# Graph convolutions: 126 of every 128 edge rows gathered by GpSimd, the last two fetched by SyncE

## The chip, the cores and the metric

The kernel runs on one core of a Trainium2 chip. The metric is the device time of one execution in microseconds (us). Engines are named as in the profile: PE is TensorE, DVE is VectorE, ACT is ScalarE, POOL is GpSimd and SP is SyncE; a "q" behind a name (SPq, POOLq) is the sequencer of that engine, which issues transfers, loads registers and waits.

## The reference

There are N = 6250 nodes with D = 512 features and E = 100000 edges, sorted by destination. First comes a graph attention layer, then two graph convolution layers, each of this form (W is 512x512):

```python
h = x @ W
deg = segment_sum(ones, dst) + 2.0
dinv = rsqrt(deg)
msgs = h[src] * (dinv[src] * dinv[dst])[:, None]
agg = segment_sum(msgs, dst) + h * (2.0 * dinv * dinv)[:, None]
x = relu(agg + b)
```

So each of the two convolutions has to read one row of 512 floats (2 KB) for each of the 100000 edges, by the edge's source, and to add it to the row of the edge's destination.

## The kernel before

The nodes are 49 tiles of 128 rows. The edges are J = 782 chunks of P = 128 edges; two chunks are a unit, and there are UNITS = 391 units. A convolution is two stages. A dense stage (`dense_layer`, L1561) makes x @ W tile by tile, already scaled, and SP writes it to a table in HBM (`h2_tab` for the first convolution, `h3_tab` for the second; the profile calls both h_tab), L1164. Then comes the aggregation stage, in which this change lies:

- **POOL** (`gather`, L1286 to L1303) issues one indirect transfer per chunk. It brings 128 rows of the table, named by a column of `src_group`, into one slot of `gcn_ring`, one row for each of the 128 partitions. The ring holds RING[1] = 12 units, which is 24 slots or six pairs of units. From the seventh pair on POOL waits, before each pair, until PE has used the pair six earlier (`step_sum`). The step numbers to wait for come from `ends_row`, 16 of them in one register load (L1293). The profile puts the gathers down to L1301.
- **SP** (`count_rows`, L1113 to L1118) waits for each pair's transfers (`rows_in`, one semaphore for each of the six places of the ring) and adds two to `rows_ready`.
- **ACT** (`make_group_onehots`) makes one-hot matrices of the destinations, for groups of four steps.
- **PE** (`aggregate`, L1713 to L1731) works through 440 steps (a constant that the code, too, calls SP); a step is one unit against one tile of destinations, so there are 49 more steps than units. Before each group of four steps it waits for `rows_ready` (that all units of the group have landed) and for the one-hots. Each step is a matmul of 128x128 by 128x512 in fp32 for each of its two chunks, which the profile shows as four records.
- **DVE** (L909) adds the finished steps to the accumulators in SBUF. In the second aggregation it also finishes tiles, and ACT writes them out and loads rows of `x1_tab` (L1530, L1536).

Before the first aggregation SP issues the loads of two biases and of the second weight matrix (L1179 to L1183); before the second it issues twelve loads of 256 KB each from `x1_tab` (L1196). During the two aggregations it has nothing to do but `count_rows`. The attention stage has a gather of the same kind (from v_tab), and that call isn't touched.

Of the kernel before, what the change touches and what calls it, by code (L numbers as in the profile page):

```python
# [8 lines left out]
I32 = mybir.dt.int32  # L9
# [3 lines left out]
ds = bass.ds  # L13

P = 128
# [3 lines left out]
TILES = -(-N // P)  # L19
NP = TILES * P  # L20
LAST = N - (TILES - 1) * P
J = -(-E // P)
# [24 lines left out]
UNITS = J // 2  # L47
# [5 lines left out]
SP = CUT.steps  # L53
# [4 lines left out]
ENDS = 16  # L58
LAG = 2
OFFS = 8  # L60
WORD = 1023
# [32 lines left out]
W_EXTRA = 2 * GE * H  # L94
XR = 4
SHORT = 3
SETTLED = UNITS
BIG = 1e38
EPS = 1e-5
# [30 lines left out]
def build(nc, x, src, dst, W_src, b_src, W_dst, b_dst, W_val, b_val, attn_l, attn_r, W1, b1, W2, b2, out):  # L130
    ctx = ExitStack()
    with ctx:
        def sb(name, shape, dt=F32):
            return ctx.enter_context(nc.sbuf_tensor(name, shape, dt))
# [4 lines left out]
        def sem(name):  # L139
            return ctx.enter_context(nc.semaphore(name))  # L140

        def dram(name, shape, dt=F32):
            return nc.dram_tensor(name, shape, dt, kind="Internal").ap()


        src_rows = dram("src_rows", [GROUPS, GE], I32)
# [13 lines left out]
        h2_tab = dram("h2_tab", [NP, D])  # L160
        h3_tab = dram("h3_tab", [NP, D])
# [31 lines left out]
        eler_hots = sb("eler_hots", [P, TILES * 2 * H])  # L193
# [3 lines left out]
        ends_row = sb("ends_row", [1, UNITS + 1], I32)  # L197

        src_group = sb("src_group", [P, J], I32)
# [24 lines left out]
        gcn_ring = edge[:, 0:2 * RING[1] * D].rearrange("p (s n) -> p s n", n=D)  # L224
# [3 lines left out]
        onehot = hots[:, :].rearrange("p (b c n) -> p b c n", b=HOTS, c=2)  # L228
        group_hots = hots[:, :].rearrange("p (g e n) -> p g e n", g=HOTS // GROUP, n=P)
        dist = eler_hots[:, 0:4 * P].rearrange("p (b c n) -> p b c n", b=2, c=2)  # L230
        stat = big[:, TILES * D:TILES * (D + 6)].rearrange("p (t s) -> p t s", s=6)
        ln = small[:, 0:4, :]
        iota_i = small[:, 4:7, :].rearrange("p s t -> p (s t)")[:, 0:P].bitcast(I32)
        W_src_sb = wmat[:, :, 0:D]
        rows = rows_w[:, :, 0:D]
# [96 lines left out]
        def first(t):  # L332
# [15 lines left out]
        ends_kept, tabs_kept, tabs_in, chunks_in = map(sem, ("ends_kept", "tabs_kept", "tabs_in", "chunks_in"))  # L348
        pad_set, const_set, ident_set, edges_kept, fold_in, edges_in, dst_in = map(sem, (
            "pad_set", "const_set", "ident_set", "edges_kept", "fold_in", "edges_in", "dst_in"))  # L350
# [12 lines left out]
        v_kept = [sem(f"v_kept{n}") for n in range(4)]  # L363
        el_in = [sem("el_in0"), sem("el_in1")]
        stepdst_in = sem("stepdst_in")
        er_in, w_kept = map(sem, ("er_in", "w_kept"))
# [3 lines left out]
        lasts_in, counted, elerT_set, eler_turned = map(sem, ("lasts_in", "counted", "elerT_set", "eler_turned"))  # L370
# [5 lines left out]
        ht_kept, low_before = low_in, [16 * len(range(n, KEPT, HT)) for n in range(HT)]  # L376
        gcn_rows_in = [sem(f"gcn_rows_in{u}") for u in range(RING[1] // 2)]
        gat_rows_in = [sem(f"gat_rows_in{u}") for u in range(RING[0])]
        agg = []
        for n, (name, c) in enumerate((("gat", 0), ("gcn1", 1), ("gcn2", 1))):  # L380
            units = RING[c]
            agg.append(dict(
                units=units, told=1 + c,
                rows_in=(gat_rows_in, gcn_rows_in)[c],
                rows_before=[32 * (n == 2) * sum(1 for g in range(UNITS) if g % units // 2 == u) for u in range(units // 2)]
                if c else [0] * units,
                rows_ready=sem(f"{name}_rows_ready"),
                dist_set=sem(f"{name}_dist_set"), onehot_set=sem(f"{name}_onehot_set"),
                step_sum=sem(f"{name}_step_sum"), acc_added=sem(f"{name}_acc_added")))
# [7 lines left out]
        mids = []  # L397
# [21 lines left out]
        def all_kept(eng, pair, per=16):  # L419
            eng.wait_ge(pair[0], per * ((TILES + 1) // 2))  # L420
            eng.wait_ge(pair[1], per * (TILES // 2))
# [3 lines left out]
            eng.wait_ge(w_placed_odd, 2 * CUT.blocks)  # L425

        waits_passed = {eng: sem(f"waits_passed_{eng}") for eng in ("pool", "dve")}

        def wait_alone(name, eng, which, value):

            eng.wait_ge(which, value)
            eng.sem_inc(waits_passed[name], 1)
# [11 lines left out]
        def _(dve):  # L444
# [513 lines left out]
            def residual(s):  # L958
                first_tiles = not s.inner and s.k < SHORT + 3
                if s.live():  # L960
                    begin_tile(s)
                if s.live(1):
                    tile_moments(s.k - 1, (s.j - 1) % 2)
                if first_tiles and 1 <= s.k <= SHORT:
                    tile_scale(s.k - 1, (s.k - 1) % 2, s.k >= 3)
                if s.live(2) and not (first_tiles and s.k - 2 < SHORT):
                    tile_scale(s.k - 2, s.j % 2, s.past(2, 2))
                if first_tiles and 2 <= s.k < SHORT + 2:
                    bank_out(mids[0], s, 2)
                if not (first_tiles and s.k - 3 < SHORT):  # L970
                    bank_out(mids[0], s, 3)
# [37 lines left out]
            def settled(k):  # L1009

                t = k - LAG - SETTLED
                if 0 <= t - 1 < TILES:
# [4 lines left out]
            dve.wait_ge(agg[2]["acc_added"], SP)  # L1017
            for k in range(SP + LAG - 1, SETTLED + LAG + TILES + 1):
                settled(k)
# [8 lines left out]
        def _(sp):  # L1028
# [32 lines left out]
            for t in range(TILES):  # L1061
                sp.wait_ge(hT_set, t + 1)
                if STAY_LO <= t < STAY_HI:
                    n = t - STAY_LO
# [48 lines left out]
            def count_rows(a):  # L1113

                for g in range(0, UNITS, a["told"]):
                    u, told = g % a["units"] // a["told"], min(a["told"], UNITS - g)
                    sp.wait_ge(a["rows_in"][u], a["rows_before"][u] + 32 * (g // a["units"] * a["told"] + told))
                    sp.sem_inc(a["rows_ready"], told)  # L1118

            def load_low(s):  # L1120
                if s.past(4):
                    sp.wait_ge(src_hot_set, (s.k - 3) * (KT - 1))
                    sp.wait_ge(far_dist, s.k - 3)
                if not s.inner and s.k in ER_LOAD:
                    n = ER_LOAD.index(s.k)
                    at = slice(n * J * H // 4, (n + 1) * J * H // 4)
                    if n == 0:
                        all_landed(sp, er_scattered, TILES)
                    sp.wait_ge(v_sum, STAY_LO)
                    sp.dma_start(er.rearrange("p j h -> p (j h)")[:, at],  # L1130
                                 er_tab[0:EP, :].rearrange("(p j) h -> p (j h)", j=J)[:, at]).then_inc(er_in, 16)
                sp.dma_start(low_all[:, s.j, :], low_tab[ds(s.k * Q, Q), :].rearrange("q n -> (q n)").rearrange(
                    "(a n) -> a n", a=1).broadcast_to([P, Q * P])).then_inc(low_in[s.j], 16)
# [4 lines left out]
            for half, at in enumerate(halves):  # L1138
                at = slice(at.start * H, at.stop * H)
# [45 lines left out]

            all_kept(sp, x1_kept)

            count_rows(agg[1])

            def between(s):  # L1190
                keep_table(mids[1], h3_tab, s, 0)
# [2 lines left out]
            sp.wait_ge(b_added, TILES)  # L1194
            for t in range(EARLY_X1):
                sp.dma_start(x1_buffer(t), x1_tab[t * P:(t + 1) * P, :]).then_inc(x1_early_in, 16)  # L1196
            count_rows(agg[2])
            sp.wait_ge(out_kept, 16 * TILES)


# [1 line left out]
        def _(pool):  # L1202
# [29 lines left out]
            for g in range(TILES // SEEK):  # L1232
# [3 lines left out]
                for t in range(g * SEEK, (g + 1) * SEEK):  # L1236
                    pool.indirect_dma_start(seek_ring[:, t % (2 * SEEK), :], None, by_row, bass.IndirectOffsetOnAxis(
                        ap=er_idx[:, t:t + 1], axis=0)).then_inc(seek_in[g % 2], 16)
# [27 lines left out]
            for t in range(TILES):  # L1266
# [8 lines left out]
                ap=dst_i[:, 0:1], axis=0)).then_inc(er_first_in, 16)  # L1275
# [7 lines left out]
                pool.indirect_dma_start(w_row_of[b], None, w_tab,  # L1283
                                        bass.IndirectOffsetOnAxis(ap=gidx[:, b:b + 1], axis=0)).then_inc(w_in[b], 16)

            def gather(tab, a, ring, done):  # L1286

                units, ends = a["units"], None
                for g in range(UNITS):
                    u, past = g % units, g - units  # L1290
                    if past >= 0:
                        if past % ENDS == 0:
                            _, ends = nc.values_load_multi_w_load_instructions(  # L1293
                                ends_row[:, past:min(past + ENDS, UNITS - units)], engines=(mybir.EngineType.Pool,),
                                min_val=1, max_val=SP, skip_runtime_bounds_check_because="clamped when the table is made")
                        if past % a["told"] == 0:
                            freed = min(past % ENDS + a["told"], len(ends)) - 1
                            wait_alone("pool", pool, done, ends[freed] & WORD)
                    for c in range(2):
                        n = 2 * g + c  # L1300
                        pool.indirect_dma_start(  # L1301
                            ring[:, 2 * u + c, :], None, tab,
                            bass.IndirectOffsetOnAxis(ap=src_group[:, n:n + 1], axis=0)).then_inc(a["rows_in"][u // a["told"]], 16)  # L1303

            pool.wait_ge(tabs_in, 64)
            pool.wait_ge(dve_prep, marks["tables"])
# [16 lines left out]
                    collect_den(t + XR)  # L1323
            pool.wait_ge(x1_set, TILES)
            all_kept(pool, mids[0]["kept"])
            gather(h2_tab, agg[1], gcn_ring, agg[1]["step_sum"])
            all_kept(pool, mids[1]["kept"])
            gather(h3_tab, agg[2], gcn_ring, agg[2]["step_sum"])


        @block.scalar
        def _(act):
# [166 lines left out]
            def residual(s):  # L1499
                first_tiles = not s.inner and s.k < SHORT + 2  # L1500
                if s.live(1):
# [36 lines left out]
            def settled(q):  # L1538
                for t in range((q - 4) * GROUP - SETTLED, (q - 3) * GROUP - SETTLED):
                    if 0 <= t < TILES:  # L1540
                        out_and_x1(t)
            make_group_onehots(agg[2], settled)
            for t in range((SP // GROUP - 4) * GROUP - SETTLED, TILES):
                out_and_x1(t)
# [233 lines left out]
```

## Time and profile before

| what | value |
|---|---|
| device time, three runs | 4063.41, 4064.51 and 4065.05 us, median 4064.51 us |
| profiled execution | 4065.91 us, of which 4064.1 us are its span (first to last instruction) |
| busy shares of the span | PE 85%, POOL 66%, DVE 55%, ACT 44% |
| gathers of the two convolutions (L1301, h_tab) | 1564 of them, 1482.5 us busy, 948 ns each |
| first aggregation, its gathers | from 1856.69 us on, 782 of them |
| second aggregation, its gathers | from 3046.16 us on, the last one issued at 4026.08 us |
| all DMA | 789.67 MB, mean 194 GB/s |

The page shows the span in 40 slices of about 102 us. Slices 19 to 28 are the first aggregation, slices 31 to 40 the second. In them POOL's digit is 7, PE's is 8, and DMA moves 210 GB/s. A busy share isn't yet a bound: for each stage one has to ask who waits for whom, and at what interval the instructions of the slowest engine start. Times of one instruction are in ns.

### The profile page before, as it was taken

The numbers are of one execution on the slowest core, as the hardware profiler recorded it, in microseconds if no ns is written. First come the engines' busy times: TensorE is split into PE (matmuls) and PEld (weight loads), VectorE is DVE, ScalarE is ACT, GpSimd is POOL, SyncE is SP. The second block draws the span as 40 slices with busy tenths as digits, with TensorE's granted clock in tenths as the row PEclk, the third lists the DMA queues.
The fourth block names the chain that finished last, engine by engine and source line by source line (L and its number), as shares of the span: only waits on it lengthen the run. The fifth ranks groups of instructions, "written<-read, shape, count | busy, mean of one in ns | idle before, by whom it ended". The sixth has DMA issues, their size and how long they took to land.

```text
span 4064.1 us, 53477 instructions
## 1 busy us (share of the span) xinstructions
PE 3446.4 (85%) x14344; PEld 1653.5 (41%) x14344; DVE 2246.1 (55%) x3787; ACT 1789.0 (44%) x4164; POOL 2666.3 (66%) x2801
## 2 busy tenths in 40 slices
PE   6899998777888888897788888889996788888887
PEld 4499943222233333443333333333442333333333
DVE  7489997777778888882223323333542222223336
ACT  4356615454455555453334434444443333334442
POOL 3676604777777777555777777776007777777774
PEclk9999999999999999998999999999998999999998
DMA  7633437777777777566777777776117777777779
GB/s 278 165 65 62 94 109 244 210 211 211 210 210 210 211 210 210 186 204 194 210 210 210 211 210 210 210 211 192 60 70 238 211 210 210 210 210 210 210 210 352
DMA packets 311566, 789.67 MB, mean 194 GB/s; under 512 B 74033, under 2 KB 97091, under 8 KB 310449
## 3 DMA queue, kind: packets, MB, share of 16 engines
q0 software_dynamic: 201856, 631.01, 54.3%
q1 hardware_dynamic: 81813, 108.37, 8.4%
q10 hardware_dynamic: 27708, 48.21, 3.4%
q8 instruction: 66, 1.08, 0.1%
q14 instruction: 123, 1.01, 0.1%
HBM read 706.27 MB, written 81.90 MB: 194 GB/s over the span
## 4 chain that ended last, share of the span: by engine, by line
PE 34%; POOL 24%; issue 21%; DMA 12%; DVE 6%; POOLq 1%; DVEq 1%; ACT 1%; ACTq 0%; SPq 0%
POOL edge L1301 18%; PE mm L1561 8%; POOL rows_wmat L1301 6%; DMA edge<-h_tab,src_group 5%; DMA rows_wmat<-v_tab,src_group 5%; PE mm L1729 4%; PE mm L1657 4%; PE tr L1657 4%; PE sm L1729 4%; PE tr L1729 3%; PE sm L1602 2%; DVE edge L882 2%; PE tr L1556 1%; PE hist_ps L1729 1%; DVE big L894 1%
## 5 line engine op out<-in xcount | busy, mean ns | idle before, releaser
L1301 POOL DMA_INDIRECT edge<-h_tab,src_group x1564 | 1482.5, 948 | 708.8 <-issue 447.2
L1468 ACT ACTIVATE hots<-iota,drel 128x128 f32<-128x128 f32 x1760 | 538.0, 388 | 1174.8 <-PE tr L1729 578.2
L1301 POOL DMA_INDIRECT rows_wmat<-v_tab,src_group x782 | 739.3, 945 | 258.8 <-issue 219.3
L1729 PE MATMUL mm<-edge,hots 128*128 x880 | 448.7, 658 | 185.7 <-SPq L1118 177.1
L1729 PE MATMUL sm<-edge,hots 128*128 x880 | 460.8, 673 | 158.3 <-SPq L1118 158.3
L909 DVE TENSOR_TENSOR big<-big,mm 128x512 f32 x220 | 151.2, 687 | 658.9 <-PE tr L1729 639.9
L909 DVE TENSOR_TENSOR big<-big,sm 128x512 f32 x220 | 151.2, 687 | 630.9 <-PE misc L1729 616.9
L1729 PE MATMUL tr<-edge,hots 128*128 x880 | 395.6, 592 | 0.0
L1729 PEld LDWEIGHTS mm<-edge,hots 128*128 128x128 f32 x880 | 177.1, 209 | 450.1 <-issue 450.1
L1729 PEld LDWEIGHTS sm<-edge,hots 128*128 128x128 f32 x880 | 182.7, 215 | 428.3 <-issue 428.2
L1561 PE MATMUL mm<-rows_wmat 128*128 128x512 f32 x784 | 356.6, 599 | 0.0
L1709 PE MATMUL mm<-edge,hots 128*128 128x512 f32 x592 | 277.3, 608 | 59.0 <-ACT hots L1450 39.3
L1709 PE MATMUL sm<-edge,hots 128*128 128x512 f32 x584 | 275.9, 602 | 54.9 <-issue 28.3
L882 DVE TENSOR_TENSOR edge<-rows_wmat,tr 128x1024 f32<-128x1024 f32 x224 | 272.0, 1215 | 81.9 <-SPq L1118 80.2
L882 DVE TENSOR_TENSOR edge<-rows_wmat,misc 128x1024 f32<-128x1024 f32 x216 | 262.6, 1216 | 80.7 <-SPq L1118 80.6
L1450 ACT ACTIVATE hots<-eler_hots,ones 128x256 f32<-128x256 f32 x440 | 223.6, 508 | 186.7 <-PE sm L1709 68.1
L1445 ACT ACTIVATE eler_hots<-iota,drel 128x128 f32<-128x128 f32 x880 | 298.2, 386 | 0.0
L1260 POOL DMA_INDIRECT edge<-el_tab,src_flat x222 | 212.6, 958 | 99.7 <-issue 56.1
L1471 ACT ACTIVATE hots<-hots,ones 128x1024 f32<-128x1024 f32 x220 | 252.6, 1148 | 7.1
L1729 PEld LDWEIGHTS tr<-edge,hots 128*128 128x128 f32 x880 | 167.6, 190 | 212.3 <-issue 212.3
L1729 PE MATMUL hist_ps<-edge,hots 128*128 x440 | 206.8, 592 | 0.0
L1729 PE MATMUL misc<-edge,hots 128*128 x440 | 206.8, 592 | 0.0
(262 smaller groups left out, 4424.8 us busy)
## 6 DMA issues: line engine op xcount, KB each, us to landing
h_tab<-rows_wmat SPq DMA_DIRECT2D x98, 256.0 KB, 2.0
edge<-h_tab,src_group POOLq DMA_INDIRECT x1564, 3.7
rows_wmat<-low_tab SPq DMA_DIRECT2D x140, 128.0 KB
v_tab<-rows_wmat ACTq DMA_DIRECT2D x49, 256.0 KB, 2.9
x_tab<-big SPq DMA_DIRECT2D x49, 256.0 KB, 2.1
rows_wmat<-v_tab,src_group POOLq DMA_INDIRECT x782, 3.7
edge<-x SPq DMA_DIRECT2D x48, 256.0 KB
out<-big ACTq DMA_DIRECT2D x48, 256.0 KB
```

The source lines that it names most:

```text
L882: dve.tensor_tensor(msgs[:, k % MSGS, :, :].rearrange("p c (h f) -> p c h f", f=F), got, weights.unsqueeze(3).to_broadcast([P, 2, H, F]), ...
L909: dve.tensor_tensor(big[:, ds(o, D)], big[:, ds(o, D)], agg_ps[bank][:, :], ALU.add).then_inc(a["acc_added"], 1)
L1260: pool.indirect_dma_start(el[:, at, :], None, el_tab, bass.IndirectOffsetOnAxis(ap=src_flat[:, at:at + 1], axis=0)).then_inc(el_in[n // AH ...
L1301: pool.indirect_dma_start(ring[:, 2 * u + c, :], None, tab, bass.IndirectOffsetOnAxis(ap=src_group[:, n:n + 1], axis=0)).then_inc(a["rows_ ...
L1445: act.activation(dist[:, n % 2, c, :], iota[:, :], ACT.Abs, bias=drel[:, n * 2 + c:n * 2 + c + 1], scale=-1.0).then_inc(a["dist_set"], 1)
L1450: act.activation(onehot[:, n % HOTS, :, :], dist[:, n % 2, :, :], ACT.Relu, bias=ones[:, 0:1], scale=-1.0).then_inc(a["onehot_set"], 1)
L1468: act.activation(group_hots[:, q % 2, e, :], iota[:, :], ACT.Abs, bias=drel[:, col:col + 1], scale=-1.0).then_inc(a["dist_set"], 1)
L1471: act.activation(group_hots[:, q % 2, :, :], group_hots[:, q % 2, :, :], ACT.Relu, bias=ones[:, 0:1], scale=-1.0).then_inc(a["onehot_set"], 1)
L1561: last = nc.tensor.matmul(bank, rows[:, slot, k * P:(k + 1) * P], rhs(k), start=(k == 0), stop=(k == KC - 1))
L1657: last = pe.matmul(sum_ps[bank][:, q * NA * H:(q + 1) * NA * H], src_hot[:, par, kt, q * P:(q + 1) * P], el_parts[:, part, kt, :, :], star ...
L1709: last = pe.matmul(gat_ps[w % GAT_SUMS][:, :], onehot[:, w % HOTS, n, :], msgs[:, w % MSGS, n, :], start=(n == 0), stop=(n == 1))
L1729: last = pe.matmul(agg_ps[bank][:, :], group_hots[:, q % 2, w % GROUP * 2 + n, :], edge[:, ds(slot[w % OFFS] + n * D, D)], start=(n == 0), ...
```

## The change

In both convolutions POOL's indirect transfer brings only the first 126 rows of a chunk (partitions 0 to 125). SP fetches the rows of partitions 126 and 127 with one plain transfer each, whose source row is a register. For this SP loads the sources of the last two edges of every chunk from HBM into one partition (`own_ids`, in two halves of 392 and 390 chunks, the second in the middle of a stage), and from there loads them into registers, eight for a pair of units. `fetch(k)` issues the eight transfers of pair k; from the seventh pair on it first waits, as POOL does, until PE has used the pair six earlier. `relay(k)` takes the place of `count_rows`: it waits for POOL's transfers and for SP's own, and then adds to `rows_ready`. SP does four fetches ahead, and then relay(k) and fetch(k + 4) in turn. The semaphores of its own transfers are ones that earlier stages had used.

```diff
+BY_SYNC = 2
+BY_POOL = P - BY_SYNC
+PAIRS_AHEAD = 4
+UNIT_PAIRS = -(-UNITS // 2)
+IDS_HALF = J // 2 + 1
...
+        own_ids = eler_hots[0:1, 0:IDS_HALF * BY_SYNC].bitcast(I32)
...
+            def fetch_and_count_rows(a, tab, again):
+
+                pairs = a["units"] // 2
+                chunk_src = src_rows.rearrange("g (c e) -> (g c) e", e=P)
+                halves_in, ends_held, ends = [2 * again], [-1], [None]
+
+                def load_ids(half):
+                    lo = half * IDS_HALF
+                    n = min(IDS_HALF, J - lo)
...
+                        sp.dma_start(own_ids[:, 0:n * BY_SYNC].rearrange("a (c e) -> a c e", e=BY_SYNC),
+                                     chunk_src[lo:lo + n, BY_POOL:P].rearrange("(a c) e -> a c e", a=1)).then_inc(ids_in, 16)
+                    halves_in[0] += 1
+                    sp.wait_ge(ids_in, ids_before + 16 * halves_in[0])
+
+                def fetch(k):
+                    first_chunk, chunks = 4 * k, min(4, J - 4 * k)
+                    if first_chunk % IDS_HALF == 0:
+                        load_ids(first_chunk // IDS_HALF)
+                    if k >= pairs:
+                        past = 2 * (k - pairs) + 1
+                        if past // ENDS != ends_held[0]:
+                            ends_held[0] = past // ENDS
+                            _, ends[0] = nc.values_load_multi_w_load_instructions(
+                                ends_row[:, past // ENDS * ENDS:min((past // ENDS + 1) * ENDS, UNITS)],
...
+                        sp.wait_ge(a["step_sum"], ends[0][past % ENDS] & WORD)
+                        sp.sem_inc(waits_passed["sp"], 1)
+                    at = first_chunk % IDS_HALF * BY_SYNC
+                    _, ids = nc.values_load_multi_w_load_instructions(
+                        own_ids[:, at:at + chunks * BY_SYNC], engines=(mybir.EngineType.SP,), min_val=0, max_val=NP - 1,
...
+                    for c in range(chunks):
+                        for e in range(BY_SYNC):
+                            sp.dma_start(gcn_ring[BY_POOL + e:BY_POOL + e + 1, 4 * (k % pairs) + c, :],
+                                         tab[ds(ids[c * BY_SYNC + e], 1), :]).then_inc(own_in[k % pairs], 16)
+
+                def relay(k):
+                    u, turn, told = k % pairs, k // pairs, min(2, UNITS - 2 * k)
+                    sp.wait_ge(a["rows_in"][u], a["rows_before"][u] + 32 * (2 * turn + told))
...
+                    sp.wait_ge(own_in[u], own_before[u] + 16 * BY_SYNC * (before + 4 * turn + 2 * told))
+                    sp.sem_inc(a["rows_ready"], told)
+                for k in range(PAIRS_AHEAD):
+                    fetch(k)
+                for k in range(UNIT_PAIRS):
+                    relay(k)
+                    if k + PAIRS_AHEAD < UNIT_PAIRS:
+                        fetch(k + PAIRS_AHEAD)
...
-            count_rows(agg[1])
+            all_kept(sp, mids[0]["kept"])
+            fetch_and_count_rows(agg[1], h2_tab, 0)
...
-            count_rows(agg[2])
+            fetch_and_count_rows(agg[2], h3_tab, 1)
...
-            def gather(tab, a, ring, done):
+            def gather(tab, a, ring, done, n_rows=P):
...
-                            ring[:, 2 * u + c, :], None, tab,
-                            bass.IndirectOffsetOnAxis(ap=src_group[:, n:n + 1], axis=0)).then_inc(a["rows_in"][u // a["told"]], 16)
+                            ring[0:n_rows, 2 * u + c, :], None, tab,
+                            bass.IndirectOffsetOnAxis(ap=src_group[0:n_rows, n:n + 1], axis=0)).then_inc(a["rows_in"][u // a["told"]], 16)
...
-            gather(h2_tab, agg[1], gcn_ring, agg[1]["step_sum"])
+            gather(h2_tab, agg[1], gcn_ring, agg[1]["step_sum"], BY_POOL)
...
-            gather(h3_tab, agg[2], gcn_ring, agg[2]["step_sum"])
+            gather(h3_tab, agg[2], gcn_ring, agg[2]["step_sum"], BY_POOL)
```

## Rows read from the trace of the kernel before

**Rows 1.** The page: chain that ended last, by engine; gathers' median us to landing.

```profile
PE 34%; POOL 24%; issue 21%; DMA 12%; DVE 6%; POOLq 1%; DVEq 1%; ACT 1%; ACTq 0%; SPq 0%
...
edge<-h_tab,src_group POOLq DMA_INDIRECT x1564, 3.7
```

**Rows 2.** Windows: inside each aggregation, and the second one's last part.

```profile
core 0: us, PE busy (x) PEld busy (x) DVE busy (x) ACT busy (x) POOL busy (x), PEclk, DMA share, GB/s
2000.00:2800.00 800.00, 679.36 (x1458) 285.70 (x1457) 248.47 (x362) 324.85 (x815) 605.04 (x641) 0.95 0.74 210
...
3960.00:4020.00 60.00, 50.69 (x104) 21.07 (x103) 38.86 (x70) 21.60 (x55) 45.97 (x47) 0.90 0.97 360
```

**Rows 3.** POOL's indirect transfers by line, whole span: busy us, mean ns.

```profile
L1301 POOL DMA_INDIRECT edge<-h_tab,src_group x1564 | 1482.5, 948 | 708.8 <-issue 447.2 <-DMA h_tab<-rows_wmat 233.0 <-PE tr L1729 10.4
...
L1260 POOL DMA_INDIRECT edge<-el_tab,src_flat x222 | 212.6, 958 | 99.7 <-issue 56.1 <-DVE rows_wmat L705 30.5 <-DMA el_tab<-eler_hots 13.2
```

**Rows 4.** Timeline of POOL in the second aggregation: start, us.

```profile
3238.70 0.95 POOL L1301 DMA_INDIRECT edge<-h_tab,src_group  x1 [0.30 <-issue]
3239.95 0.94 POOL L1301 DMA_INDIRECT edge<-h_tab,src_group  x1 [0.30 <-issue]
```

**Rows 5.** Line L1283, gathers of 128 rows of 8 KB: ns min/median/max.

```profile
L1283 POOL DMA_INDIRECT big<-w_tab,gidx x2: 1429/1432/1434, 635.4 to 637.1; - x2
```

**Rows 6.** Timeline of PE in the second aggregation, two groups of steps.

```profile
3273.76 3.70 PE L1729 MATMUL mm<-edge,hots 128*128 x8 [2.52 <-SPq L1118]
3277.30 3.60 PE L1729 MATMUL tr<-edge,hots 128*128 x8
3283.75 3.69 PE L1729 MATMUL sm<-edge,hots 128*128 x8 [2.85 <-SPq L1118]
```

**Rows 7.** Waits of SP's sequencer: total us, times, longest.

```profile
SPq L1118 <- DMA edge<-h_tab,src_group: 1937.1, 391, 8.2
```

**Rows 8.** Timeline of SP: transfers into one partition.

```profile
518.91 0.24 SPq L1105 DMA_DIRECT2D ends_row<-ends_tab  x1
519.21 0.25 SPq L1107 DMA_DIRECT2D src_flat<-slot_tab_gat  x1
519.50 0.25 SPq L1107 DMA_DIRECT2D src_flat<-slot_tab_gcn  x1
```

**Rows 9.** Timeline of SP: transfers whose address is a register.

```profile
1696.29 0.35 SPq L1170 DMA_DIRECT2D x_tab<-big  x1
1696.84 0.35 SPq L1153 DMA_DIRECT2D edge<-x  x1
```

**Rows 10.** By line, ns min/median/max: loads of 8 and 16 registers, SP's semaphore instructions.

```profile
L1720 PEldq TENSOR_LOAD <-src_flat x110: 586/589/856, 1848.0 to 4025.9; - x110
L1293 POOLq TENSOR_LOAD <-ends_row x73: 303/1055/1622, 664.3 to 3983.5; - x73
...
L1118 SPq EVENT_SEMAPHORE  x783: 17/17/19203, 645.2 to 4032.2; - x196
```

**Rows 11.** SP before the second aggregation: issues (timeline), time to landing (line).

```profile
3045.92 6.83 SPq L1196 DMA_DIRECT2D rows_wmat<-x_tab  x12
...
DMA to landing us min/median/max: 2.7/7.8/12.7
```

**Rows 12.** Line L1110: issue of a load of 220 single words.

```profile
L1110 SPq DMA_DIRECT2D src_flat<-need_tab x1: 867/867/867, 519.8 to 519.8; - x1
```

**Rows 13.** Timelines: first gather and first matmuls of each aggregation.

```profile
1856.69 0.96 POOL L1301 DMA_INDIRECT edge<-h_tab,src_group  x1 [20.80 <-DMA h_tab<-rows_wmat]
...
1869.31 5.54 PE L1729 MATMUL mm<-edge,hots 128*128 x8 [16.14 <-SPq L1118]
...
3046.16 0.94 POOL L1301 DMA_INDIRECT edge<-h_tab,src_group  x1 [212.17 <-DMA h_tab<-rows_wmat]
...
3061.43 5.11 PE L1729 MATMUL mm<-edge,hots 128*128 x8 [18.20 <-SPq L1118]
```

**Rows 14.** Timelines of the second aggregation's last part: POOL, ACT's sequencer.

```profile
3953.70 1.23 POOL L1301 DMA_INDIRECT edge<-h_tab,src_group  x1 [0.30 <-issue]
3955.24 1.29 POOL L1301 DMA_INDIRECT edge<-h_tab,src_group  x1 [0.30 <-issue]
...
4000.51 2.81 ACTq L1536 DMA_DIRECT2D rows_wmat<-x_tab  x1
```

More of the change, by code:

```diff
@@ L378, in build @@
         gat_rows_in = [sem(f"gat_rows_in{u}") for u in range(RING[0])]
+        own_in, ids_in = v_kept + [w_kept, edges_kept], chunks_in
+        own_before, ids_before = [16 * len(range(n, TILES, 4)) for n in range(4)] + [32, 64], 32
         agg = []
@@ L427, in build @@
         waits_passed = {eng: sem(f"waits_passed_{eng}") for eng in ("pool", "dve")}
+        waits_passed["sp"] = lasts_in
         def wait_alone(name, eng, which, value):
@@ L1118, in count_rows @@
                     sp.sem_inc(a["rows_ready"], told)
+            def fetch_and_count_rows(a, tab, again):
[5 more added lines that the diff above has]
+                    n = min(IDS_HALF, J - lo)
+                    with nc.allow_non_contiguous_dma(reason="sources of the last edges of every chunk"):
+                        sp.dma_start(own_ids[:, 0:n * BY_SYNC].rearrange("a (c e) -> a c e", e=BY_SYNC),
[12 more added lines that the diff above has]
+                                ends_row[:, past // ENDS * ENDS:min((past // ENDS + 1) * ENDS, UNITS)],
+                                engines=(mybir.EngineType.SP,), min_val=1, max_val=SP,
+                                skip_runtime_bounds_check_because="clamped when the table is made")
+                        sp.wait_ge(a["step_sum"], ends[0][past % ENDS] & WORD)
[3 more added lines that the diff above has]
+                        own_ids[:, at:at + chunks * BY_SYNC], engines=(mybir.EngineType.SP,), min_val=0, max_val=NP - 1,
+                        skip_runtime_bounds_check_because="rows of the edges' sources")
+                    for c in range(chunks):
[5 more added lines that the diff above has]
+                    sp.wait_ge(a["rows_in"][u], a["rows_before"][u] + 32 * (2 * turn + told))
+                    before = again * len(range(u, UNIT_PAIRS, pairs)) * 4 - again * 2 * (u == (UNIT_PAIRS - 1) % pairs)
+                    sp.wait_ge(own_in[u], own_before[u] + 16 * BY_SYNC * (before + 4 * turn + 2 * told))
[6 more added lines that the diff above has]
+                        fetch(k + PAIRS_AHEAD)
```

## The prediction

> **What bounds the kernel now.** I read the page's chain first. PE leads it, but POOL and "issue" together have more, 45% [rows 1], so PE's busy share says little by itself. The windows split the aggregation stages from the rest: in 800 us of the first one PE is busy for 679 us and POOL for 605 us, and neither is full [rows 2]. The timeline of POOL settles it: a gather starts every 1.25 us, 0.95 us of work and 0.30 us of "issue", with no wait [rows 4]. Two starts are 1.25 us apart; 782 of them make 977.5 us, which is the length of either aggregation up to its last gather (1564 gathers and their mean: [rows 3]). PE's timeline shows the other side: a group of four steps takes some 7.1 us, and then PE waits 2.5 to 2.9 us for SP's count, with a new group every 10 us [rows 6]. SP in its turn waits for the landing of each pair, 1937 us in all [rows 7]. So the pace is POOL's price for one gather, and a pair of units (four gathers) takes 5.00 us. Is it POOL's own work or the transfer? The gathers from el_tab, in a stage where hardly anything else moves, have the same 0.95 us though their rows are 64 times smaller [rows 3], and the 16 DMA engines are 74% busy beside the gathers [rows 2]. It is POOL's own work.
>
> **What is taken away from POOL.** Two of 128 rows in each of 1564 gathers. No row of the trace shows a gather of fewer than 128 rows, so the saving is bounded. Below: nothing, if the price goes by the instruction. Above: the whole 948 ns go by the row, 2 / 128 of it is 14.8 ns, in all 23 us. Between them lies the nearest price of more work for each row: rows of 8 KB cost 1432 ns [rows 5], 484 ns more than the 948, which is 3.8 ns for each of 128 rows. Two rows fewer at that price save 7.6 ns, times 1564 that is 12 us. I take -12. PE does not cap this: its 7.1 us stand against 10.
>
> **What SP has to do for a pair**, against 5.00 us:
> - A transfer into one partition is issued every 0.29 us [rows 8]. A register as its address adds work: between two such transfers lie 0.55 us from start to start, of which 0.35 us are the first one [rows 9]; 0.05 us of the rest are in the 0.29 already, so 0.15 us come on top. Eight transfers at 0.44 us are 3.52 us.
> - The register load of eight sources: 0.59 us and a gap, 0.64 us; the load of 16 step numbers, 1.06 us, in one pair of eight: 0.14 us [rows 10].
> - Three waits, two semaphore increments and the masking of a step number, at 17 ns each [rows 10] and gaps of about 40 ns: some 0.26 us.
>
> The sum is 4.56 us, so SP keeps up, but with 0.44 us to spare. From both sides: at 0.29 us a transfer (registers free) it is 3.4 us; at the full 0.55 us of the 128-partition form it is 5.4 us. I take 4.56 us, since [rows 8] have the shape, and [rows 9] only the register. What is behind SP: relay(k + 1) stands behind fetch(k + 4), so PE learns of a pair up to 4.6 us late, and PE's steps set the ring free for POOL. In the steady state this is covered: POOL can be 24 gathers (30.0 us) ahead of the pair whose place it wants. A pair is complete 5 us of gathers and 3.7 us of landing [rows 1] after its first gather, may wait 5 us for the rest of its group, and takes up to 7.1 us, 20.8 us together. So SP may be some 9 us behind at no price.
>
> **The start of each aggregation** isn't covered. SP now loads the sources, does four fetches of 4.3 us (without relay), then relay(0), fetch(4) and relay(1), and only then can PE's first group start. Before, it started 12.6 us after the first gather in the first aggregation, 15.3 us in the second [rows 13].
> - First aggregation: the load of 392 pairs of words is issued in about 1.2 us (220 words took 0.87 us [rows 12]) and lands after some 4 us; together 5. Then 17.2 + 4.5 us, and relay(1) is at 26.7 us. PE's first two steps take 5.5 us at its clock after the pause [rows 13]: the first pair's place is free at 32.4 us, and POOL wants it at 30.0 us. Price +2 us, bounds 0 and +7.
> - Second aggregation: the twelve loads of L1196 stand ahead. They are issued at 3052.75 us, 6.6 us after the first gather, and land a median 7.8 us later [rows 11]. The sources land behind them, at about 15.6 us. Then relay(1) is at 37.3 us, and the place is free at 42.5 us. Price +12 us, bounds +8 and +15.
>
> After each of these stalls SP gains 0.44 us on POOL in each pair and has its reserve back after some 20 to 30 pairs. The second half of the sources is loaded in the middle of a stage, some 6 us beside running gathers, inside the 9 us of reserve: +1 for each stage, bounds 0 and +5. In the last 70 us of the second aggregation ACT's stores and loads take the DMA engines to 97% [rows 2], gathers grow to 1.29 us, and an issue on ACT's queue takes up to 2.8 us [rows 14]. SP's 120 small transfers of these pairs go into the same crowd: +3 us, bounds 0 and +10.
>
> **Sum:** -12 + 2 + 12 + 2 + 3 = +7 us on the profiled execution's 4065.9 us, 4072.9 us. The median of the runs lies 1.4 us below that execution, so I predict 4071.5 us. The ends of this case are -23 + 8 = -15 (4049) and 0 + 30, some 4095 us.
>
> **A rule on how the rows are dealt out.** The trace has only 128-row gathers. By the Trainium skill ("DMA: Bandwidth & Descriptors", the section on why a DMA increments its semaphore by 16) a transfer runs on the largest number of engines, up to 16, that divides its slowest dimension. By that rule 128 rows are 8 on each of 16 engines, and 126 rows are 9 on each of 14; and one-partition transfers from SP would all use the lowest-numbered engine. No row here shows either. What each would make of the time is worked out from rows in the second and the fourth rival.
>
> **The rivals.**
> 1. *SP becomes the pace* (slower). It needs 0.495 us a transfer instead of 0.44, since (5.00 - 1.04) / 8 = 0.495; or waits for PE's steps of 0.44 us a pair. At 5.2 us a pair it costs 196 pairs x 2 x 0.2 = 78 us on top of about 17: 4160 us; at the full 0.55 us of [rows 9], 5.4 us, +157 us. For it speak the thin margin, and that fetch(k + 4) needs the steps of pair k - 2, which at times are only the first of the group that relay(k) lets go; against it that [rows 8] show the very shape of transfer. Chance 0.22.
> 2. *A gather of 126 rows costs more than one of 128* (slower). An even deal of 126 rows reaches at most 14 of 16 engines, 9 rows each; if POOL deals evenly and works in waves of one row for each engine, 9 waves take the place of 8. The part that grows with rows is about 484 ns [rows 3, 5]; an eighth of it is 61 ns, x 1564 = +95 us, and with the starts (which then are partly hidden) some 4170 us. For it: 126 isn't a multiple of 16. Against it: nothing in the trace. The rule of the Trainium skill told above gives the same 9 rows, but no time for them. Chance 0.17.
> 3. *A gather gets clearly cheaper* (faster). If the same 484 ns go by the DMA engine served and two of them fall out, the sign is turned: -61 ns, -95 us, and +19 for the rest: 3988 us. SP's 4.56 us a pair would still pass under the 4.76 us that POOL then takes, but barely. It decides from about 17 ns saved in each gather. Chance 0.13.
> 4. *One DMA engine becomes the bound* (slower). The engines are busy for 0.74 of 1.25 us, 0.93 us a gather [rows 2]. If all of SP's rows run on one engine (the rule told above names the lowest-numbered one), it gets two more rows beside its eight: 10 / 8 of 0.93 us is 1.16 us, under 1.25 us, so it shouldn't decide outside the last 70 us. At 1.30 us a gather it would cost 78 us. Chance 0.06.
>
> The forecast's own case, SP keeps up and the gather's price hardly moves, has the remaining 0.42.
>
> **How the numbers follow.** The measurement tells 0.2%, 8.1 us, from no change. The forecast's case (4049 to 4095 us) gives 0.07 to faster, 0.22 to same and 0.13 to slower. With rival 3 faster has 0.20; same has 0.22; with rivals 1, 2 and 4 slower has 0.58. The range leaves out most of rival 3 (0.12) and the far ends of the slow ones (0.08): 4045 to 4180 us.
>
> **What the profile after would show.** The start-to-start time of POOL's gathers in mid-stage: 1.24 us by the forecast; 1.25 or more, or under 1.23, speak for rivals. SP's eight transfers start 0.44 us apart and leave it waiting at the relay for POOL's landing; if it never waits there, and POOL waits for steps throughout, it is rival 1. POOL's seventh pair starts about 2 us late in the first aggregation and 12 us late in the second. The gathers' packets and the busy share of the engines show rivals 2 and 4. I am wrong above all if an issue costs SP over 0.495 us, or if the price of a gather jumps at other than 128 rows in either direction.

## The result, and the profile after

The changed kernel takes 4172.84 us (median of 5 runs, 4168.59 to 4177.62), the kernel before 4064.51 us (5 runs, 4059.89 to 4067.98). The ratio is 1.0266, with an interval of 1.0254 to 1.0278: 108 us slower. The profiled execution has a span of 4171.0 us, 106.9 us more than before.

POOL's rows of the page by line show it at once (busy us and mean ns; compare [rows 3]): the gathers of 126 rows are dearer, not cheaper, while those of 128 rows from v_tab and el_tab cost what they did. There is also idle time before them for which PE is named. The last line is the v_tab row of the kernel before.

```profile
L1362 POOL DMA_INDIRECT edge<-h_tab,src_group x1564 | 1534.8, 981 | 749.9 <-issue 442.2 <-DMA h_tab<-rows_wmat 232.3 <-PE mm L1790 41.9
L1362 POOL DMA_INDIRECT rows_wmat<-v_tab,src_group x782 | 739.4, 946 | 257.9 <-issue 224.5 <-DVE big L864 20.0 <-DVE edge L891 13.4
L1321 POOL DMA_INDIRECT edge<-el_tab,src_flat x222 | 212.7, 958 | 98.8 <-issue 55.8 <-DVE rows_wmat L714 31.1 <-DMA el_tab<-eler_hots 11.8
...
L1301 POOL DMA_INDIRECT rows_wmat<-v_tab,src_group x782 | 739.3, 945 | 258.8 <-issue 219.3 <-DVE big L855 20.9 <-DVE edge L882 18.6
```

POOL's timeline tells where the 107 us are. The rows are, in order: the first gather and the 24th and 25th of the first aggregation, two of its middle, its last; then the first, 24th and 25th of the second, two from its last part, and its last (start us, us; in brackets the idle time before).

```profile
1855.57 1.00 POOL L1362 DMA_INDIRECT edge<-h_tab,src_group  x1 [20.81 <-DMA h_tab<-rows_wmat]
...
1885.15 0.99 POOL L1362 DMA_INDIRECT edge<-h_tab,src_group  x1 [0.30 <-issue]
1893.15 0.97 POOL L1362 DMA_INDIRECT edge<-h_tab,src_group  x1 [7.01 <-PE mm L1790]
...
2301.51 0.97 POOL L1362 DMA_INDIRECT edge<-h_tab,src_group  x1 [0.30 <-issue]
2302.79 0.99 POOL L1362 DMA_INDIRECT edge<-h_tab,src_group  x1 [0.30 <-issue]
...
2865.25 0.99 POOL L1362 DMA_INDIRECT edge<-h_tab,src_group  x1 [0.30 <-issue]
...
3077.69 0.97 POOL L1362 DMA_INDIRECT edge<-h_tab,src_group  x1 [211.45 <-DMA h_tab<-rows_wmat]
...
3107.20 0.99 POOL L1362 DMA_INDIRECT edge<-h_tab,src_group  x1 [0.30 <-issue]
3137.58 0.97 POOL L1362 DMA_INDIRECT edge<-h_tab,src_group  x1 [29.40 <-PE mm L1790]
...
4099.74 0.99 POOL L1362 DMA_INDIRECT edge<-h_tab,src_group  x1 [0.30 <-issue]
4106.53 0.97 POOL L1362 DMA_INDIRECT edge<-h_tab,src_group  x1 [5.80 <-PE sm L1790]
...
4118.44 0.99 POOL L1362 DMA_INDIRECT edge<-h_tab,src_group  x1 [0.30 <-issue]
```

In mid-stage two starts are 1.284 us apart (mean of gathers 300 to 600 of either aggregation) where they were 1.250 us. The 25th gather, the first one that needs a place set free, comes 8.00 us after the 24th in the first aggregation and 30.38 us in the second, which is 6.7 and 29.1 us too late. From the last gather to the end of the span it was 38.0 us, and is 52.6 us. So the 106.9 us divide as follows:

| part | us |
|---|---|
| first aggregation, 781 steps of 34 ns more | +26.6 |
| first aggregation, late 25th gather | +6.7 |
| second aggregation, 781 steps of 34 ns more | +26.6 |
| second aggregation, late 25th gather | +29.1 |
| second aggregation, what is left (waits in its last 70 us) | +5.1 |
| behind the last gather | +14.6 |
| up to the first gather, and between the aggregations | -1.8 |

SP's timeline shows both starts (start us, us from the first to the last of a group). In the first aggregation the sources are issued at 1854.85 us and SP's first transfer starts at 1866.45 us; in the second, behind the twelve loads of L1257 (L1196 before), 3084.04 us and 3109.68 us.

```profile
1854.85 0.82 SPq L1139 DMA_DIRECT2D eler_hots<-src_rows  x1
1866.45 17.46 SPq L1164 DMA_DIRECT2D edge<-h_tab  x33
...
3077.43 6.57 SPq L1257 DMA_DIRECT2D rows_wmat<-x_tab  x12
3084.04 0.84 SPq L1139 DMA_DIRECT2D eler_hots<-src_rows  x1
3109.68 20.08 SPq L1164 DMA_DIRECT2D edge<-h_tab  x40
```

What SP's own work costs is in the rows by line (ns min/median/max): a transfer is issued in 220 ns, its register work takes 37 and 29 ns more, and from start to start it is 0.40 us. The load of eight registers takes 0.69 us. One fetch without waits is 4.1 us.

```profile
L1164 SPq FUSED_REGOPS  x3128: 37/37/47, 1866.3 to 4125.4; - x196
L1164 SPq MOVE edge<-h_tab x3128: 29/29/40, 1866.4 to 4125.5; - x196
L1164 SPq DMA_DIRECT2D edge<-h_tab x3128: 213/220/616, 1866.4 to 4125.5; - x196
...
L1159 SPq TENSOR_LOAD <-eler_hots x392: 462/689/1866, 1865.5 to 4123.7; - x196
```

And SP's waits (us in total, times, longest). It now waits for matmuls in `fetch` (L1157; the two rows below and 25 us for other banks, 210 us in all) and for POOL's rows only 72 times in 392 relays, 72 us, where `count_rows` waited 1937 us [rows 7]. SP is nearly always a few us behind. The page's chain that ended last now has 18% of the span on SP's sequencer, where it had 0% [rows 1]. That alone would speak for the first rival, SP as the pace; e1 and e6 test it.

```profile
SPq L1157 <- PE mm L1790: 97.8, 37, 9.3
SPq L1157 <- PE sm L1790: 87.2, 39, 10.1
SPq L1172 <- DMA edge<-h_tab,src_group: 72.0, 72, 5.8
```

### The profile page after: what moved, and what is told of

It reads as the page before. It is cut to its first block, busy times and chain, and to the rows that moved or that the text cites. A ratio compares the mean times of both kernels' runs of the same rounds, so it can differ in the third digit from the quotient of the medians.

```text
span 4171.0 us, 64066 instructions
## 1 busy us (share of the span) xinstructions
PE 3443.1 (83%) x14344; PEld 1648.9 (40%) x14344; DVE 2249.1 (54%) x3787; ACT 1789.2 (43%) x4164; POOL 2718.8 (65%) x2801
## 4 chain that ended last, share of the span: by engine, by line
PE 34%; issue 20%; SPq 18%; POOL 10%; DMA 9%; DVE 6%; DVEq 1%; ACT 1%; ACTq 0%; POOLq 0%
SPq L1164 12%; PE mm L1622 8%; POOL edge L1362 5%; PE mm L1790 5%; POOL rows_wmat L1362 5%; PE sm L1790 5%; DMA rows_wmat<-v_tab,src_group 4%; PE mm L1718 4%; PE tr L1718 4%; SPq L1159 4%; PE sm L1663 2%; DMA edge<-h_tab,src_group 2%; DVE edge L891 2%; PE tr L1790 2%; PE tr L1617 1%
## 5 line engine op out<-in xcount | busy, mean ns | idle before, releaser
L1362 POOL DMA_INDIRECT edge<-h_tab,src_group x1564 | 1534.8, 981 | 749.9 <-issue 442.2
L1790 PE MATMUL sm<-edge,hots 128*128 x880 | 449.4, 658 | 179.4 <-SPq L1172 168.3
```

What stands on the lines that cost most here:

```text
L1362: pool.indirect_dma_start(ring[0:n_rows, 2 * u + c, :], None, tab, bass.IndirectOffsetOnAxis(ap=src_group[0:n_rows, n:n + 1], axis=0)).the ...
L1790: last = pe.matmul(agg_ps[bank][:, :], group_hots[:, q % 2, w % GROUP * 2 + n, :], edge[:, ds(slot[w % OFFS] + n * D, D)], start=(n == 0), ...
```

## The experiments

Ratios are to the kernel before on the same chip. Each edit is given as a diff against the kernel that its expectation names.

**e1, 126 rows without SyncE.** Does the dearer gather come from its row count or from SP's traffic beside it?

```diff
-                            ring[:, 2 * u + c, :], None, tab,
-                            bass.IndirectOffsetOnAxis(ap=src_group[:, n:n + 1], axis=0))
+                            ring[0:n_rows, 2 * u + c, :], None, tab,
+                            bass.IndirectOffsetOnAxis(ap=src_group[0:n_rows, n:n + 1], axis=0))
...
-            gather(h2_tab, agg[1], gcn_ring, agg[1]["step_sum"])
+            gather(h2_tab, agg[1], gcn_ring, agg[1]["step_sum"], 126)
```

> The kernel before, but GpSimd gathers 126 rows in both convolutions and nobody fetches the other two (partitions 126 and 127 of the ring keep what was in them, so two edges in 128 are wrong). Theory A: a gather of 126 rows itself costs 34 ns more than one of 128, without any help of SyncE: starts 1.284 us apart, no stall at the start, 1564 x 34 ns = +53 us, about 4118 us. Rival B: the 34 ns come from SyncE's transfers beside it: starts 1.25 us apart or a little less, 4050 to 4065 us.

Measured: 4130.46 us, ratio 1.0160 (1.0143 to 1.0177). Its row by line has the changed kernel's price:

```profile
L1301 POOL DMA_INDIRECT edge<-h_tab,src_group x1564 | 1535.3, 982 | 709.8 <-issue 446.4 <-DMA h_tab<-rows_wmat 233.1 <-PE tr L1729 12.2
```

Starts are 1.284 us apart and there is no late 25th gather. Theory A holds: the 34 ns belong to the gather of 126 rows. The time is 12 us more than it gave, though: behind the last gather it is 53.3 us here too, 15.3 us more than before, with not one transfer of SP's in it. So with 126 rows the stretch behind the last gather is as long without SP's transfers. The gathers of the second aggregation themselves have only 0.8 us beyond the 34 ns a gather, and no two starts over 2.2 us apart, where the changed kernel has 5.1 us and a gap of 6.8 us. e5 takes the last part up.

**e2, 120 rows; e3, 112 rows; e9, 124 rows; e10, 96 rows**, all without SyncE. The edit is that of e1 with another number.

> As e1, with 120 rows a gather (the last 8 edges of each chunk left out). Waves theory (the price goes by the rows for each of the DMA engines that an even deal reaches: 15 engines with 8 rows each): as for 128, 1.250 us from start to start, no change. Rival, an extra price for any number of rows that isn't a multiple of 16: about 1.26 to 1.29 us. Rival, by the row: 8 rows fewer at 3.8 ns, 1.22 us.

> As e1, with 112 rows a gather (the last 16 edges of each chunk left out), 16 engines with 7 rows each. Waves theory: one wave of 34 to 61 ns less than 128 rows, 1.19 to 1.216 us from start to start, time down by 53 to 95 us. If the price goes by the instruction alone it stays at 1.25 us.

> As e1, with 124 rows a gather (the last 4 edges of each chunk left out). An even deal of 124 rows reaches 4 engines, 31 rows each. If the extra price is one for any number that isn't a multiple of 16, 1.29 us from start to start as with 126 and 120 rows. If it goes by the rows that an engine gets (7, 8, 8, 9 in the runs so far), 31 rows would make it several times dearer, 1.5 us or more, or the transfer itself (31 rows on one engine at some 84 ns) sets a pace of its own.

> As e1, with 96 rows a gather (the last 32 edges of each chunk left out), 16 engines with 6 rows each. From 128 to 112 rows the price fell by 21 ns, 1.3 ns a row. A straight line gives 1.208 us from start to start; PE's steps are still shorter (0.9 us a gather), so it should show in the time: about 4008 us, 28 us less than with 112.

Measured, with the time of one run each, and the mean distance of starts for gathers 300 to 600 of the first aggregation. The last column is arithmetic, the even deal over at most 16 engines.

| rows | start to start, us | POOL's ns | time, us | even deal |
|---|---|---|---|---|
| 128 (before) | 1.250 | 948 | 4064.51 | 16 x 8 |
| 126 (e1) | 1.284 | 982 | 4130.46 | 14 x 9 |
| 124 (e9) | 1.591 | 1287 | 4608.13 | 4 x 31 |
| 120 (e2) | 1.282 | 979 | 4128.46 | 15 x 8 |
| 112 (e3) | 1.229 | 928 | 4036.05 | 16 x 7 |
| 96 (e10) | 1.216 | 914 | 4010.96 | 16 x 6 |

The rows by line of 120, 112 and 124 rows, each of its own run:

```profile
L1301 POOL DMA_INDIRECT edge<-h_tab,src_group x1564 | 1530.9, 979 | 712.7 <-issue 447.4 <-DMA h_tab<-rows_wmat 232.3 <-PE sm L1729 11.9
```

```profile
L1301 POOL DMA_INDIRECT edge<-h_tab,src_group x1564 | 1451.7, 928 | 709.2 <-issue 444.3 <-DMA h_tab<-rows_wmat 233.0 <-PE mm L1729 8.2
```

```profile
L1301 POOL DMA_INDIRECT edge<-h_tab,src_group x1564 | 2013.0, 1287 | 718.9 <-issue 443.8 <-DMA h_tab<-rows_wmat 235.2 <-PE sm L1729 15.4
```

Multiples of 16 get cheaper with fewer rows, though slowly: 21 ns for the first 16 rows (1.3 ns a row), 13 ns for the next. The other numbers pay extra. The waves of e2 and e3 don't explain it: 120 rows are no more for each engine than 128 and cost 32 ns more. That the number isn't a multiple of 16 doesn't explain it alone either: 124 rows cost 341 ns more than 128. It is POOL's own busy time that grows there, 948 to 1287 ns, so it isn't the transfer that sets the pace.

So in e2 the rival held (1.26 to 1.29 us), in e3 neither value came (1.19 to 1.216 us or 1.25), in e9 it was the rows for each engine (1.5 us or more), and e10 came within 8 ns of its straight line.

The queue rows of the page (packets, MB) show that the deal itself changes. First the kernel before, then e1:

```profile
q0 software_dynamic: 201856, 631.01, 54.3%
```

```profile
q0 software_dynamic: 226880, 624.71, 53.6%
```

25024 packets more for 1564 gathers are 16 more for each, with fewer bytes. Inside the aggregation the trace has 14 packets of 2048 and 56 of 4096 bytes a gather in place of 64 of 4096: 9 rows for each of 14 engines. The Trainium skill's rule told in the prediction (the engines are the largest number up to 16 that divides the rows) agrees. The trace also has 26 packets of 4 or 8 bytes a gather where there were 16, and some 208 of them in e9.

These small packets follow a count. The 16 of before are still 16 with 112 and 96 rows. Each engine that the deal leaves out adds one small packet for each packet of rows that a served engine has: 2 x 5 with 126 rows, 1 x 4 with 120, 12 x 16 with 124. Together the packets of one left-out engine hold 4 bytes for each row that a served engine gets. So it looks as if GpSimd wrote a place for every engine, served or not: 144 places with 126 rows, 128 with 120, 496 with 124. From 144 to 496 places POOL's time grows by 305 ns, which is 0.87 ns a place; among the multiples of 16 it is 0.9 and 1.3 ns a row. What is left over is a step of 31 ns as soon as an engine is left out (120 rows have 128 places, like 128 rows). By this estimate 126 rows would cost 993 ns, and they cost 982. It is a count that fits the runs, and the trace doesn't name the engines; no run separates the two parts.

**e4, sources loaded early.** The first half is issued behind the attention stage, and again right behind the first aggregation; SP waits for it at its first fetch.

```diff
+            fetch_and_count_rows(agg[1], h2_tab, 0, only_ids=True)
...
             fetch_and_count_rows(agg[1], h2_tab, 0)
+            fetch_and_count_rows(agg[2], h3_tab, 1, only_ids=True)
```

> The changed kernel, but the first half of the sources is loaded long before each aggregation (behind the attention stage, and right behind the first aggregation). Theory: the seventh pair's late start of 6.7 us in the first aggregation goes to 0, that of 29 us in the second to 2 to 6 us (SyncE still issues the twelve loads of x1 first): 30 us less than the changed kernel, about 4142 us. Rival: the late start is made good later by SyncE's lag, and the time moves by under 10 us.

Measured: 4141.26 us, ratio 1.0184 (1.0167 to 1.0201), against 1.0266 of the changed kernel. The late start of the first aggregation is gone (1.29 us from the 24th to the 25th gather), that of the second is 6.2 us:

```profile
3101.64 0.99 POOL L1369 DMA_INDIRECT edge<-h_tab,src_group  x1 [0.30 <-issue]
3109.14 0.97 POOL L1369 DMA_INDIRECT edge<-h_tab,src_group  x1 [6.52 <-PE mm L1797]
```

The theory holds, and nothing of the starts is made good later.

**e5, the last 28 pairs by GpSimd alone.**

```diff
+OWN_PAIRS = (UNIT_PAIRS_ALL, 168)
...
-            gather(h3_tab, agg[2], gcn_ring, agg[2]["step_sum"], BY_POOL)
+            gather(h3_tab, agg[2], gcn_ring, agg[2]["step_sum"], lambda g: BY_POOL if g < 2 * OWN_PAIRS[1] else P)
...
-                    if k + PAIRS_AHEAD < UNIT_PAIRS:
+                    if k + PAIRS_AHEAD < OWN_PAIRS[again]:
```

> The changed kernel, but in the second aggregation from pair 168 of 196 on GpSimd gathers all 128 rows and SyncE fetches none. After the changed kernel's last gather came 52.6 us (38.0 before), and its last 60 us of gathers hold stalls of 7 us; e1 without SyncE's fetches has 53.3 us. Theory: it is the gathers of 126 rows that make the crowded last part dear, so with 128 rows the stretch behind the last gather goes back to about 40 us and the stalls to what they were: 20 us less and 4 us for 112 cheaper gathers, about 4149 us. Rival: the last part is later because what runs in front of it is out of step, whatever the rows: no more than the 4 us, about 4169 us.

Measured: 4150.24 us, ratio 1.0207 (1.0190 to 1.0224). Behind the last gather it is 39.9 us, and the 7 us stall is gone, though the late start in front of it was the largest of all (31.11 us between two starts). So the theory holds, and what stands in front of the last part doesn't make it long. The crowded last part is best seen in the windows, 30 us of it in e1, in the changed kernel and in e5, where 1.05, 1.05 and 1.04 of the DMA engines' time move 323, 337 and 407 GB/s; before it was 408 GB/s at 1.04 in the same part.

```profile
4047.00:4077.00 30.00, 15.11 (x28) 6.17 (x27) 12.16 (x22) 5.08 (x15) 21.18 (x22) 0.80 1.05 323
```

```profile
4091.00:4121.00 30.00, 15.53 (x28) 6.28 (x27) 12.46 (x22) 5.27 (x15) 17.75 (x18) 0.80 1.05 337
```

```profile
4071.00:4101.00 30.00, 24.58 (x51) 10.27 (x50) 19.50 (x36) 10.17 (x27) 22.99 (x24) 0.89 1.04 407
```

In the same part of e3 (112 rows) and e10 (96 rows), where the deal is even over 16 engines, it is 357 and 355 GB/s:

```profile
3954.00:3984.00 30.00, 26.71 (x55) 11.18 (x54) 20.57 (x37) 14.03 (x36) 22.99 (x24) 0.89 1.04 357
```

```profile
3929.00:3959.00 30.00, 24.45 (x51) 10.01 (x50) 18.87 (x34) 10.79 (x27) 22.77 (x24) 0.89 1.05 355
```

So the same full engines move less with every number of rows tried other than 128: a fifth less with 126 and with 120 rows (325 GB/s in e2), but also an eighth less with 112 and 96. An uneven deal can't be the whole reason. A mean packet of 4096 bytes took 161 ns in that window before and in e5, 189 ns in e3, 184 in e10, 212 in e2 and 208 in e1; ACT's packets of 2048 bytes took 85 ns before and 105 in e1. Why isn't shown. The Trainium skill ("DMA: Bandwidth & Descriptors", the descriptor swizzle) states that in a transfer of 128 partitions each engine writes one port of SBUF; a deal of nine rows would cross those groups of partitions, and so might one of seven or six. No run here separates that from other reasons.

SP's transfers aren't free there in general. With 112 rows beside them the stretch behind the last gather is 48.4 and 48.7 us (e8, e11), against 41.1 us without them (e3), one run each. The stretch also varies by itself: it is 39.9 us in e5 and 33.7 us in e7, both with 128 rows at the end.

**e6, three pairs ahead.**

```diff
-PAIRS_AHEAD = 4
+PAIRS_AHEAD = 3
```

> The changed kernel with PAIRS_AHEAD 3 instead of 4. The first relay comes one fetch (4.1 us) earlier in each aggregation, and fetch(k + 3) needs the steps of a pair that is one further back, so SyncE's 210 us of waits for matmuls should fall below 50 us. Theory (GpSimd's price sets the pace, SyncE's waits are hidden): only the two starts gain, 2 x 4.1 us, about 4164 us; from start to start of a gather it stays 1.284 us. Rival (SyncE's loop is what holds the pace): the gathers close up to under 1.28 us, and it gains 30 us or more.

Measured: 4163.49 us, ratio 1.0247 (1.0230 to 1.0264). Both 25th gathers are some 5 us less late, mid-stage stays at 1.284 us, and SP's waits for matmuls shrink from 210 us to the two rows below, while it waits for POOL at 284 relays:

```profile
SPq L1172 <- DMA edge<-h_tab,src_group: 266.1, 284, 4.9
...
SPq L1157 <- PE mm L1790: 11.3, 1, 11.3
SPq L1157 <- PE sm L1790: 4.4, 1, 4.4
```

The theory holds: with 126 rows SP doesn't set the pace, in either form, whatever the chain's share of SP says.

**e7, e4 to e6 together.**

> The changed kernel with the sources loaded early, three pairs ahead and the last 28 pairs by GpSimd alone. Theory: nothing of the starts and of the last part is left, only 34 ns for each of 1452 gathers of 126 rows, +49 us on the kernel before: 4114 us. If there is another cost that the terms don't have, it is above 4120 us.

Measured: 4119.16 us, ratio 1.0130 (1.0113 to 1.0147). It is 5 us over the expected 4114 us. The expectation had forgotten a late 25th gather, 6.7 us in the second aggregation: the twelve x1 loads still stand before SP's first fetch. It is the best form of this split that was run, and 54 us slower than the kernel before.

**e8 and e11, 112 rows by GpSimd and two by SyncE.** Where would SP become the pace? The kernels are e4's with 112 in place of 126, with four and with three pairs ahead.

> As e4, but GpSimd gathers only 112 rows and SyncE the last two; partitions 112 to 125 are left out. e3 had 1.229 us from start to start with SyncE idle, which is 4.92 us a pair. SyncE needs about 4.6 us a pair and waits for matmuls besides. Theory: SyncE keeps up here too, 1.229 us in mid-stage, 4045 to 4055 us. Rival (SyncE's loop has 5.1 us a pair): 1.26 to 1.29 us from start to start, about 4100 us.

> As e8 (112 rows by GpSimd, two by SyncE, the rest left out) with three pairs ahead instead of four. In e8 the gathers stalled 10 times in the first aggregation, and SyncE waited 210 us for matmuls. Theory: those waits are what made SyncE's loop too long; with them gone SyncE needs about 4.3 us a pair against 4.92, the stalls go, mean 1.23 us in both aggregations, about 4045 us. Rival: SyncE's own issuing is too slow for 4.92 us a pair, and it stays near 4086 us.

Measured: e8 4086.40 us and e11 4057.78 us, one run each. In e8 most gathers are 1.229 us apart, but the mean is 1.254 us over the first aggregation, with twelve gaps of 1.6 to 6.5 us between two starts, such as this one:

```profile
2352.10 0.93 POOL L1369 DMA_INDIRECT edge<-h_tab,src_group  x1 [0.31 <-issue]
2358.57 0.92 POOL L1369 DMA_INDIRECT edge<-h_tab,src_group  x1 [5.55 <-PE mm L1797]
```

Seven of them stand at the same gathers in the second aggregation too (the 172nd, 232nd, 240th, 284th, 400th, 464th and 492nd), so the layout of the edges has to do with them. In e11 there is none in mid-stage (mean 1.232 us). SP's own work is some 4.2 us a pair, and with four pairs ahead it waits for matmuls of a pair too near for another 0.54 us (211 us in 392 pairs): together 4.74 us, close enough to 4.92 us that a run of long waits can empty the ring. With three pairs ahead it keeps up. The theory of e8 fell, that of e11 holds for mid-stage; its time is 13 us over, mostly from a second start that is 9.6 us late and 48.7 us behind the last gather.

## Why the prediction was right in its direction and where its sum failed

- *What bounds the kernel*: right. POOL's price for a gather is the pace, before and after; 112 and 96 rows made the kernel 29 and 53 us faster without another edit.
- *What is taken away from POOL*: this term failed. The step was to take 3.8 ns a row from the gathers of 8 KB rows and to let both bounds lie at or under zero, -12 us. It measured 34 ns more a gather, +53 us. A row itself is worth 1.3 ns (128 to 112 rows), so two rows save 4 us in all; the 3.8 ns were a price of longer rows, not of more of them. The term's bounds, 0 and -23 us, left out that a gather of fewer rows could be dearer; that stood in rival 2 alone.
- *Rival 2* is what happened in kind: a gather of 126 rows costs more than one of 128. Its size was 61 ns against a measured 34, and its reason, nine waves in place of eight, is not the cause as it stands: 120 rows keep eight and cost 32 ns. Rival 3, the same amount with the other sign, is out.
- *SP's work*: 0.44 us a transfer was predicted and 0.40 measured, 4.3 us a fetch and 4.1 measured. SP kept up (rival 1 is out), but its reserve didn't grow back by 0.44 us a pair as the text had it: waits for matmuls, 210 us, took most of it. They cost nothing at 1.284 us a gather (e6); at 1.229 us they did (e8 against e11).
- *The starts*: the mechanism was right, the size was not, +6.7 and +29.1 us against +2 and +12. The mis-sized term is the landing of the sources. Until SP's first register load, 9.8 us went by behind the issue in the first aggregation and 23.9 us in the second (predicted 3.8 and about 8). The 392 pieces of eight bytes stand behind the weights (1.5 MB), or behind the twelve loads of x1 (3 MB), in the same queue and beside the gathers. In mid-stage, with gathers beside it but nothing of that kind in front, a load of the same form kept SP waiting 4.4 us at most. The median to landing of one load [rows 11] was the wrong row for a transfer that comes behind all twelve.
- *The second half of the sources*: +1 us for each stage was predicted, nothing was measured; no two starts in mid-stage are more than 1.43 us apart.
- *The last part*: +3 us was predicted, +19.7 us measured (5.1 + 14.6), and in the main not for the reason given. e1 has 16.1 of it (0.8 + 15.3) without one transfer of SP's, and it goes when the last 112 gathers have 128 rows (e5). So the gathers of 126 rows are the cause of most of it. The other 3.6 us aren't divided: SP's transfers may be in them, but e2 has a stall of 5.6 us there without them.
- *One engine as the bound* (rival 4): the profile has no times by engine here, but e1 without SP's transfers has the same mid-stage price, so they don't set it. Each of them has one packet of 2048 bytes and one of 4, so it does run on a single engine.
- The chance of 0.58 on slower and the range up to 4180 us held the result because rivals 1 and 2 each reached it; the likeliest time, 4071.5 us, missed it by 101 us. That the 4170 us of rival 2 come so near is luck: its price of the gathers is 42 us too high, and the starts and the last part make that up. The range's upper end is also no sum of the terms: their upper bounds add up to +42 us, where the text has +30.

What stays open: whether the extra price of a gather divides as the count of places has it, with a step for any engine left out; and why packets take longer in a crowd with any other number of rows than 128.

## What to carry to other kernels

The price of an indirect transfer on GpSimd went in steps with the number of partitions, and sixteen decides: a multiple of 16 saved 1.3 ns a row at most, and the other numbers tried (126, 124, 120) cost 32 to 341 ns more than 128 rows. Before work is moved off an engine, the smaller form of its instruction should be measured by itself, here one run of a kernel that leaves two rows out. And what a helper engine needs first (indices, registers) belongs in front of the stage: a small load behind 3 MB of others in its own queue landed 24 us after its issue, and nothing made that good.

## What the runs showed of the hardware that wasn't expected

- GpSimd's indirect transfer of 2 KB rows, from start to start: 1.250 us for 128 rows, 1.284 for 126, 1.591 for 124, 1.282 for 120, 1.229 for 112, 1.216 for 96.
- 126 rows make 16 more packets a gather than 128, ten of them of 4 or 8 bytes. Full DMA engines moved 323 to 337 GB/s with such gathers in the mix, 355 to 357 with gathers of 96 or 112 rows, 407 with gathers of 128 rows.
- SyncE issues a 2 KB transfer into one partition, at an address from a register, every 0.40 us, while the DMA engines move 205 GB/s in all.
